# A Mamba block with a gated feed-forward layer: the first layer norm computed transposed, and the last VectorE tap of the convolution given to ScalarE and GpSimd

## The reference

```python
xz = x @ W_in.T; x_ssm, z = split(xz)              # 128 -> 2 x 256 channels
x_ssm = silu(causal_depthwise_conv(x_ssm, 4 taps) + conv_b)
B, C, dt = x_ssm @ W_x.T; dt = softplus(dt * W_dt + b_dt)
h = exp(dt * A) * h + (x_ssm * dt) * B             # scan over 256 positions, 256 channels x 16 states
y = (sum over states of h * C + x_ssm * D) * silu(z)
x = layernorm(x + y @ W_out.T)                     # the first norm, over 128 channels, eps 1e-5
g = silu(x @ w1 * s1) * (x @ w2 * s2)              # 128 -> 512
g = gelu(g @ h1 * s1'); g = gelu(g @ h2 * s2')     # 512 -> 512, twice
x = layernorm(x + g @ w3 * s3)                     # the second norm
```

## Time and profile before

| | |
|---|---|
| median of 3 runs | 1017.27 us (1015.03 to 1018.2) |
| the profiled execution, time | 1015.19 us |
| the profiled execution, span | 1013.3 us |
| busy share: PE, VectorE, ScalarE, GpSimd | 95%, 92%, 86%, 87% |
| granted TensorE clock, mean | 0.98 of full speed |

### The profile page before, as it was taken

How to read it: one execution, slowest core, us unless ns; L and a number is a source line. 1 busy time by engine, 2 the same in 40 slices (tenths; PEclk the granted TensorE clock), 3 DMA queues, 4 the chain that set the end, 5 groups by cost and what they waited for, 6 DMA issues and landing times.

```text
span 1013.3 us, 13725 instructions
## 1 busy us (share of the span) xinstructions
PE 960.7 (95%) x3874; PEld 427.7 (42%) x3874; DVE 931.6 (92%) x1117; ACT 871.7 (86%) x1497; POOL 877.6 (87%) x529
## 2 busy tenths in 40 slices
PE   7947899999999999999999999999999999989998
PEld 3313335353444435344443535344443534434454
DVE  3799999999999999999999999999999999999500
ACT  5396899999999999999999999999999999987341
POOL 3588998989999898999999899999989899979420
PEclk9686999999999999999999999999999999999999
DMA  6969395794939497693949679493939769393000
GB/s 213 246 184 283 100 279 146 203 247 118 285 95 281 123 246 201 161 276 98 279 102 270 163 205 245 125 275 104 296 104 250 197 164 270 98 277 81 1 11 11
DMA packets 110718, 185.18 MB, mean 183 GB/s; under 512 B 12977, under 2 KB 23729, under 8 KB 110641
## 3 DMA queue, kind: packets, MB, share of 16 engines
q1 hardware_dynamic: 110112, 183.98, 68.6%
q10 hardware_dynamic: 528, 0.32, 0.1%
HBM read 162.23 MB, written 22.02 MB: 182 GB/s over the span
## 4 chain that ended last, share of the span: by engine, by line
issue 44%; DVE 41%; PE 10%; POOL 3%; ACT 1%; DVEq 0%; DMA 0%; POOLq 0%; ACTq 0%
DVE hb L865 21%; DVE U L854 16%; PE GY L951 6%; POOL pb L407 2%; DVE gT L805 1%; DVE conv L794 1%; DVE x L810 1%; PE GY L942 1%; PE GY L1008 1%; PE GY L898 1%; ACT dA L515 0%; DMA win_sb<-win_d 0%; PE GY L983 0%; PE GY L958 0%; PE GY L955 0%
## 5 line engine op out<-in xcount | busy, mean ns | idle before, releaser
L407 POOL TENSOR_TENSOR pb<-hb,crep 128x1024 f32<-128x1024 f32 x256 | 602.1, 2367 | 34.8 <-DVE hb L865 30.6
L865 DVE TENSOR_TENSOR_SCAN hb<-dA,U 128x512 f32<-128x512 f32 x512 | 594.3, 1203 | 0.0
L515 ACT ACTIVATE dA<-dtr,negA 128x510 f32<-128x510 f32 x500 | 325.8, 716 | 16.7 <-DVE hb L865 15.1
L854 DVE TENSOR_TENSOR U<-X,xdr 128x512 f32<-128x512 f32 x500 | 318.3, 683 | 0.0
L951 PE MATMUL GY<-g,h_sb 128*128 128x512 f32 x512 | 234.2, 601 | 0.0
L951 PE MATMUL GY<-hid,h_sb 128*128 128x512 f32 x512 | 228.3, 599 | 1.7 <-ACT dts L583 1.0
L951 PEld LDWEIGHTS GY<-g,h_sb 128*128 128x128 f32 x512 | 93.5, 190 | 138.2 <-issue 138.2
L951 PEld LDWEIGHTS GY<-hid,h_sb 128*128 128x128 f32 x512 | 93.8, 190 | 136.5 <-issue 123.0
L942 PE MATMUL GY<-pb,sel_sb 128*32 128x512 f32 x1024 | 138.7, 614 | 11.6 <-POOL pb L407 11.6
L469 POOL TENSOR_TENSOR hid<-hid,g 128x512 f32<-128x512 f32 x64 | 80.6, 1273 | 8.7 <-ACT g L764 8.4
L958 PE MATMUL GY<-x1T,w_sb 128*128 128x512 f32 x128 | 68.2, 614 | 2.0 <-ACT hid L760 1.7
(11 more groups left out here) (135 smaller groups left out, 1068.0 us busy)
## 6 DMA issues: line engine op xcount, KB each, us to landing
dtr<-scr_dt SPq DMA_DIRECT2D x252, 256.0 KB, 8.0
xdr<-scr_xd SPq DMA_DIRECT2D x252, 256.0 KB, 7.7
brep<-scr_rows SPq DMA_DIRECT2D x32, 256.0 KB, 6.6
crep<-scr_rows SPq DMA_DIRECT2D x32, 256.0 KB, 9.1
scr_dt<-dts SPq DMA_DIRECT2D x32, 256.0 KB, 4.9
scr_xd<-xds SPq DMA_DIRECT2D x32, 256.0 KB, 5.1
xres<-xT_d SPq DMA_DIRECT2D x16, 256.0 KB, 9.6
xT_sb<-xT_d SPq DMA_DIRECT2D x15, 256.0 KB, 4.6
```

What stands on the lines that cost most here:

```text
L407: nc.gpsimd.tensor_tensor(pb[:, qs:qs + 2, :], hb[:, hs:hs + 2, :], crep[:, b % 2, g:g + 1, :].to_broadcast([P, 2, TB]), ALU.mult).then_in ...
L515: nc.scalar.activation(halves(dA[:, decay_slot(b, u), :])[:, :, 1:SEQ], halves(BREP[q] if by_product(b, k) else dtr[:, slot, q, :])[:, :, ...
L854: nc.vector.tensor_tensor(U[i][:], X[:], xdr[:, slot, q + i, :], ALU.mult).then_inc(s_u, 1)
L865: nc.vector.tensor_tensor_scan(hb[:, 2 * (v % H_PAIRS) + i, :], dA[:, decay_slot(j, u), :], U[i][:], 0.0, ALU.mult, ALU.add).then_inc(s_h, 1)
```

## The change

The first norm is computed with channels on the partitions. TensorE forms the centred sum as one 128x512 block (three products), ScalarE squares it once into a new buffer xn, TensorE sums the squares over the channels with a matrix of ones (`sum_squares`), ScalarE forms exp(-0.5*ln(var+eps)) in two passes, and VectorE multiplies straight into x1T (`norm1`, at v = 6 between the two products U and the scans). The transposes, the copy of x1T, the four accumulating squares and GpSimd's two steps of the first rsqrt go. The third tap becomes a third scaled copy by ScalarE (into xn) and a third sum by GpSimd; `taps(A)` on VectorE goes. GpSimd does its last output term of a round before the tap sums. The second z product uses another bank and moves up on TensorE; X is refilled at v = 2 where it was v = 3; both copies of z follow the squares; the SiLU of xs moves ahead of the fourth GELU; a table preload follows the first three GELUs of g2.

```diff
@@ -36,7 +36,7 @@
...
-POOL_TAPS = 2
+POOL_TAPS = 3
...
@@ -121,12 +116,11 @@
...
-        xtap0 = [hid[:, 0, :], gT[:, 1, :]]
+        xtap0 = [hid[:, 0, :], gT[:, 1, :], xn[:]]
...
-        var1, ve1, rs1 = sb("var1", [P, NT]), sb("ve1", [P, NT]), sb("rs1", [P, NT])
...
@@ -195,15 +190,18 @@
...
-        BZ = G2
-        BOUT, BX1, BW3 = Y1, Y1, G0
+        def bank_z(b, c):
+            return G0 if c == 1 and b > 2 else G2
+        BOUT, BVAR, BW3 = Y1, G2, G0
...
-        BH2_2 = GY[:, 1:3, :]
+        BH2_2 = (GY[:, 1:3, :],)
...
@@ -497,6 +491,9 @@
...
+                    if v == 15 and intake and back:
+                        for i in range(POOL_TAPS):
+                            add_tap0(I, i)
@@ -537,6 +534,10 @@
...
+                    act.wait_ge(s_x1, b - 2)
+                else:
+                    act.wait_ge(s_wop, 1)
+                    act.wait_ge(s_start, 2)
...
@@ -684,7 +683,7 @@
...
                         softplus_logs(A, 0, lambda: decay(j, 2 * v + AHEAD))
-                    if v == 3 and scan and j > 0:
+                    if v == 2 and scan and j > 0:
                         fill_X(j, 1)
@@ -701,7 +700,9 @@
...
                         act.wait_ge(s_op, F + 1)
-                        variances(x1, lambda t: tile_of(BOUT, t), var1, range(NT), s_var1)
+                        if front:
+                            act.wait_ge(s_tap0, POOL_TAPS * (A - 1))
+                        nc.scalar.activation(xn[:], BOUT, ACT.Square, scale=DM ** -0.5).then_inc(s_sq, 1)
                     if v == 8 and scan and j > 0:
@@ -713,8 +714,9 @@
...
                         if scan:
-                            gelu(g2, flat(BH2_2), s_h2, s_g2, T, 0, 2)
+                            gelu(g2, flat(BH2_2[0]), s_h2, s_g2, T, 0, 2)
                             gelu(g2, BH2[2], s_h2, s_g2, T, 2, 1)
+                            act.preload_act_table_set("natural_log_exp_and_others")
                         else:
@@ -722,18 +724,26 @@
...
                         copy_z(A, 0)
-                    if v == 4 and tail and not front:
-                        for m in ((3,) if scan else (2, 3)):
+                    if v == 4 and tail and not scan:
+                        for m in (2, 3):
                             gelu(g2, BH2[m], s_h2, s_g2, T, m, 1)
+                    if v == (3 if tail else 4) and back and front:
+                        copy_z(A, 1)
                     if v == 5 and front and not back:
...
                         act.preload_act_table_set("natural_log_exp_and_others")
-                    if v == 5 and front:
+                    if v == 5 and front and not back:
                         copy_z(A, 1)
                     if v == 5 and back:
-                        act.wait_ge(s_x1t, F + 1)
-                        nc.scalar.activation(x1T[:, F % 2, :], BX1, ACT.Copy).then_inc(s_x1c, 1)
+                        if front and not tail:
+                            act.preload_act_table_set("natural_log_exp_and_others")
+                        if j == 1:
+                            act.wait_ge(s_zero, 3)
+                        act.wait_ge(s_var1, F + 1)
+                        nc.scalar.activation(xn[:], BVAR, ACT.Ln, bias=eps[:, 0:1]).then_inc(s_ln1, 1)
+                        act.wait_ge(s_ln1, F + 1)
+                        nc.scalar.activation(xn[:], xn[:], ACT.Exp, scale=-0.5).then_inc(s_rs1, 1)
                     if v == 6:
@@ -749,13 +759,13 @@
...
                             nc.scalar.activation(yo[:, 3, :], BLAST[3][:, 0:P], ACT.Copy, scale=rs2[:, 3:4]).then_inc(s_yoa, 1)
-                        if tail and front:
+                        if front and back:
+                            act.wait_ge(s_tap0, POOL_TAPS * (A - 1))
+                            act.wait_ge(*((s_tap1, 3 * A - 6) if tail else (s_conv1, A + 1)))
+                            nc.scalar.activation(flat(xs[:, A % 2, :, :]), flat(conv[:]), ACT.Silu).then_inc(s_xs, 2)
+                        if tail and scan:
                             gelu(g2, BH2[3], s_h2, s_g2, T, 3, 1)
                         for m in range(NH) if back else ():
-                            if m == 1 and front:
-                                act.wait_ge(s_tap, taps_before(A + 1))
-                                act.wait_ge(*((s_tap1, 3 * A - 6) if tail else (s_conv1, A + 1)))
-                                nc.scalar.activation(flat(xs[:, A % 2, :, :]), flat(conv[:]), ACT.Silu).then_inc(s_xs, 2)
                             act.wait_ge(s_ga, 4 * F + 1 + m)
@@ -782,14 +792,11 @@
...
-                moved = POOL_TAPS if b > 1 else 0
-                for s in range(1, TAPS - moved):
+                for s in range(1, TAPS):
...
-                    if moved:
-                        dve.wait_ge(s_tap0, POOL_TAPS * (b - 1))
...
-                        dve.wait_ge(s_tap, taps_before(b) + s - 1)
+                        dve.wait_ge(s_tap, 3 * b + s - 1)
@@ -803,6 +810,10 @@
...
+            def norm1(b):
+                dve.wait_ge(s_rs1, b + 1)
+                nc.vector.tensor_tensor(x1T[:, b % 2, :], BOUT, xn[:], ALU.mult).then_inc(s_x1, 1)
...
@@ -852,6 +861,8 @@
...
                                 nc.vector.tensor_tensor(U[i][:], X[:], xdr[:, slot, q + i, :], ALU.mult).then_inc(s_u, 1)
+                        if v == 6 and back:
+                            norm1(F)
                         if v == 9 and tail:
@@ -866,8 +877,6 @@
...
-                    if v == 1 and front and j > 0:
-                        taps(A)
...
@@ -989,19 +998,15 @@
...
                 pe.wait_ge(s_gate, 2 * b + 2)
-                for t in range(NT):
-                    nc.tensor.matmul(tile_of(BOUT, t), tile_of(xres[:], t), cent[:], start=(t == 0), stop=False, skip_group_check=True)
-                for t in range(NT):
-                    for c in range(NC):
-                        last = nc.tensor.matmul(tile_of(BOUT, t), tile_of(gT[:, c, :], t), wout_sb[:, c, :],
-                                                start=False, stop=(c == NC - 1), skip_group_check=True)
+                nc.tensor.matmul(BOUT, cent[:], xres[:], start=True, stop=False)
+                for c in range(NC):
+                    last = nc.tensor.matmul(BOUT, wout_sb[:, c, :], gT[:, c, :], start=False, stop=(c == NC - 1))
                 last.then_inc(s_op, 1)
-            def turn_x1(b):
-                pe.wait_ge(s_x1, b + 1)
-                for t in range(NT):
-                    last = nc.tensor.transpose(tile_of(BX1, t), x1[:, t, :], ident[:])
-                last.then_inc(s_x1t, 1)
+            def sum_squares(b):
+                pe.wait_ge(s_sq, b + 1)
+                nc.tensor.matmul(BVAR, ones[:].to_broadcast([P, P]), xn[:], start=True, stop=True).then_inc(s_var1, 1)
@@ -1078,21 +1083,31 @@
...
                         z_proj(A, 0)
+                    if v == 3 and tail and front:
+                        pe.wait_ge(s_g2, 4 * T + 3)
+                        z_proj(A, 1)
                     if v == 3 and tail:
...
                         hidden(BH2[3], h2_sb, 3, g1, s_g1, s_h2, T)
-                    if v == (4 if back else 5) and front:
+                    if v == (4 if back else 5) and front and not tail:
                         pe.wait_ge(s_zc, 2 * A + 1)
...
                     if v == 4 and back:
-                        turn_x1(F)
+                        if front:
+                            pe.wait_ge(s_zc, 2 * A + 2)
+                        else:
+                            pe.wait_ge(s_g2, 4 * T + 2)
+                        pe.wait_ge(s_one, 1)
+                        sum_squares(F)
                     if v == 4 and tail:
...
                         else:
+                            if front:
+                                pe.wait_ge(s_zc, 2 * A + 2)
                             add_x1(T)
                     if v == 4 and tail and j <= NB:
-                        down(T, range(NH - 1 if front else NH))
+                        down(T, range(NH - 1 if scan else NH))
                     if v == 12 and intake and not back:
...
```

More of the change, by code:

```diff
@@ L46, in decay_slot @@
     return (TILES * b + u) % DA_RING
-def taps_before(b):
-    return 3 * b if b < 2 else 6 + (3 - POOL_TAPS) * (b - 2)
 def states_of(k):
@@ L109, in build @@
         gT = sb("gT", [P, NC, TB])
-        x1 = sb("x1", [P, NT, DM])
-        wout_raw = x1[:].rearrange("p a b -> p (a b)")[:, 0:DI]
-        diagD = x1[:].rearrange("p (a c) b -> p a c b", a=2)[:, 1, :, :]
+        xn, ones = sb("xn", [P, TB]), sb("ones", [P, 1])
+        wout_raw = xn[:, 0:DI]
+        diagD = xn[:, DI:].rearrange("p (c b) -> p c b", c=NC)
         rep_sb = gT[:, 1, 0:PARITIES * P].rearrange("p (e m) -> p e m", e=PARITIES)
@@ L144, in build @@
         s_warm = sem("s_warm")
+        s_one = sem("s_one")
         s_zero, s_aexp, s_aneg = sem("s_zero"), sem("s_aexp"), sem("s_aneg")
@@ L443, in _ @@
             nc.gpsimd.memset(eps[:], EPS).then_inc(s_zero, 1)
```

(20 more changed lines are left out.)

2 lines of the change are left out of this document (1 added, 1 removed).

## The result

**The changed kernel takes 1037.84 us (median of 4 runs, 1037.03 to 1039.29), the kernel before 1016.15 beside it: a ratio of 1.0216 [1.0199, 1.0233].** The forecast was 1034 with a range of 1012 to 1043. The profiled execution took 1037.18 us with a span of 1035.4, against 1013.3 before. One execution in what follows, of e12, took 1036.05 us with its granted clock at 0.931 where the others had 0.976 to 0.981, and e12's time leaves it out.

The account below looks back on a forecast made before the run. ScalarE and TensorE hand in hand become the bound, at 59.36 us a round against 57.84: +1.52 over 12 rounds is 18.2, with the ends +18.3, so 1015.19 becomes 1033.5, taken as 1034 (range 1012 to 1043).

Parts of the forecast that it names:

- A: ScalarE from the anchor (table load before the SiLU of xs at v = 6) to the softplus: 12.29 becomes 14.48 us.
- B: ScalarE from the softplus to the load before the first GELUs of g2: 30.40 becomes 30.76 us.
- C: ScalarE from the load before the first GELUs of g2 to the refill of X: 5.94 becomes 4.72 us.
- D: ScalarE from the refill of X to the next round's table load at v = 6: 9.21 becomes 9.40 us.
- GpSimd ... priced at nothing: GpSimd's added sum of 1.29 us a round was priced at nothing: 56.3 us of work lies under VectorE's 57.21.
- The square's step: The norm's one square on ScalarE was taken as 0.50 us, between bounds of 0.48 and 0.61.
- the anchor of round 2: Round 2's table load at v = 6 was to come 0.5 us earlier than in the kernel before.
- Behind the last anchor: After the last such load, the norm's product adds 0.6 us; the stretch after the last scan was priced at 0.
- VectorE's idle time: About 2.1 us a round, before the U product of step 4 and at step 12, waiting for ScalarE's X.
- VectorE's floor: Rival, chance 0.16: VectorE stays the bound at 57.21 us a round, giving 1006 us.
- The handshake costs half: Rival, chance 0.12: ScalarE and TensorE wait less at v = 6; round 58.0 to 58.8 us, 1018 to 1027 us.
- Switches close together cost more: Rival, chance 0.04: three nearby table loads cost a further 1.28 us a round, giving 1049 us.

Follow-up runs that it names:

- e12: e9 with the norm's Ln and Exp moved ahead of the last decay of step 5 on ScalarE; 1013.58 us, ratio 0.9966.
- e3: The changed kernel with the third tap given back to VectorE; 1024.33 us, ratio 1.0078.
- e8: The changed kernel with gate 1 waiting for one tap sum instead of three, and round 0's sums behind output term 15; 1034.70 us.
- e7: e1 with gate 1 waiting for one tap sum instead of three, and round 0's sums behind output term 15; 1014.93 us.
- e9: e7 with the table load after the first three GELUs of g2 moved behind the start of Y and the refill of X; 1011.02 us.
- e2: e1 with one extra table load, forced by a one-element exponential between the fourth GELU and SiLU 0; 1033.52 us.
- e6: e1 with the third tap back on VectorE, leaving the transposed norm without the extra table load; 1015.49 us, ratio 0.9990.
- e1: The changed kernel with the SiLU of xs back behind gate pair 0, so seven table loads a round instead of eight; 1017.84 us.
- e4: The kernel before with only the third tap moved (third scaled copy by ScalarE, third sum by GpSimd); 1032.32 us, ratio 1.0145.
- e5: e4 with GpSimd's three tap sums behind output term 15 instead of ahead of it; 1027.85 us, ratio 1.0110.
- e10: The changed kernel with the last part of the down-projection behind up-projection 1 on TensorE; 1057.30 us, ratio 1.0408.

## Why the prediction was right, point by point

**The round.** Forecast 59.36, measured 59.39. Its four parts:

| stretch | forecast | measured | marks of the changed kernel |
|---|---|---|---|
| A, anchor to softplus | 14.48 | 14.16 | 464.21, 478.37 |
| B, to the load before g2 | 30.76 | 30.65 | 509.02 |
| C, to the refill of X | 4.72 | 5.16 | 514.18 |
| D, to the next anchor | 9.40 | 9.42 | 523.60 |

The sum is closer than its parts deserve, which is luck: A came out 0.32 short of its forecast and C 0.44 over. *A* was 0.32 too long. I let up 1 wait for SiLU 0 and start 0.35 behind it, 6.53 after the anchor. SiLU 0 was in time, and up 1 ran on behind gate product 1 without a gap (469.58 + 0.86 = 470.44), 6.23 after the anchor. Up 3 followed 9.75 after the anchor instead of 9.97, and the softplus 4.41 behind it instead of 4.51. *C* was 0.44 too short: the third GELU of g2 waits 0.30 for GpSimd's sum, because the three tap sums now stand ahead of it, and the wait takes away an overlap of 0.11 (the two GELUs take 1.02 + 0.60 apart and 1.51 together in e3). That is the step "GpSimd ... priced at nothing", and it was wrong: I compared GpSimd's work of a whole round with the floor and did not look at its place in the round. e3 shows the term's size (0.41 of the tap's 0.99). The square's step was 0.48, within its bounds of 0.48 and 0.61.

**Start and end.** I said -0.5 at the anchor of round 2; it was +1.9. In round 0 the third sum stands ahead of the output terms for which the first gate waits, which is the same oversight. e8 and e7 do these sums later and give back 3.1 and 2.9 us. Behind the last anchor I had +0.6 and it was +1.6. The missing 1.0 lies behind the last gate of VectorE: 56.7 us (978.72 to 1035.4) where it was 55.7 (957.61 to 1013.3). I had priced one more table load there and called it even. The new form brings two, since no preload stands ahead of the last norm and its logarithm and its exponential each get a load of their own. That these loads are the missing 1.0 is read from the timeline and not tested:

```profile
986.45 1.28 ACT L744 ACT_TABLE_LOAD   x1
...
988.45 1.28 ACT L746 ACT_TABLE_LOAD   x1
```

The misses at the two ends, 2.4 and 1.0 us, are nearly all of the 3.7 between the 1033.5 forecast for the profiled execution and its 1037.18. From there to 1034 the forecast added 0.5, though it named 2.1 as the distance of the median; the measured distance is 0.66.

**The mechanism.** The tests named before came out so: the anchor every 59.4 us (yes), TensorE's wait of about 1.3 for the GELU (1.26), the softplus 14.5 after the anchor (14.16), no wait of ScalarE for a scan (none in the round). VectorE's idle time was forecast at about 2.1 and measured at 1.9 (57.48 busy of 59.39), but it is not where I put it: only 0.1 at the refill of X of step 4 and none at step 12; it stands at the two gates and at the scaling of yo. e8 shows that the place tells nothing of the cause: with gate 1's wait loosened, 0.73 of it is at the refill of X and the round is the same.

**The rivals.** VectorE's floor (1006) was excluded by its gaps, and e9, the best of its kind, still has a round of 57.61. "The handshake costs half" would have been 58.0 to 58.8. It fell because nothing caught up behind the wait: copy 1 still waits 0.24 for up 1, and the softplus waits 0.67 for TensorE where it waited 0.57 before. "Switches close together cost more" fell as well. The Trainium skill, in "ScalarE: Activation LUTs", section "What ACT_TABLE_LOAD costs", has a drain of about 1380 ns with every switch. The trace does not agree: the three loads at v = 6 take 1.30 or less each with the step to their instruction, and e2's added load costs 1.29 us a round.

**What the change is made of.** From e6 the norm's new form costs nothing when the tap stays on VectorE. The other two parts do not simply add up. The four rounds are:

| SiLU of xs | tap on VectorE | tap moved |
|---|---|---|
| behind pair 0 | 57.72 (e6) | 57.82 (e1) |
| ahead of the GELU | 58.40 (e3) | 59.39 (changed) |

With the tap moved, the place of the SiLU is worth 1.57 us a round, as much as the whole change costs in a round, and 1.29 of it is the load that the place brings (e2); with the tap on VectorE it is 0.68, because there VectorE's work alone takes 57.72, and that is the round in e6. The tap's move costs 0.99 where ScalarE sets the round, and 0.1 where it does not, though it takes 0.63 of work from VectorE. What the tap gives VectorE went to waits, first at the gate, then at X's refill, and came back in small part when a load was put behind that refill (e9).

## What to carry to other kernels

Don't read an engine's slack over the whole round: GpSimd had 3 us free and the third tap still cost 0.99 us a round (e4). Look at the place where each piece of new work goes in, on every engine that gets one. Moving GpSimd's three sums alone gave back only 0.15 (e5), since ScalarE's third copy and the refill and the norm behind it were late as well. A switch of tables costs its load where the engine's order is on the ring, so group by table, and put copies, which need none, ahead of the load rather than behind it. The largest gap of the fastest engine need not be what costs time: loosen its wait first and see if the period moves.

## What the runs showed that I had not expected

- TensorE's granted clock fell to 0.50 in the middle of eight steady rounds of e10 after idle times of 1.17 and 0.78 us with one product between them, and was back at 1.00 some 3.4 us later. That cost 1.6 to 1.7 us of slower products in such a round. In five other rounds of the same execution the same two idle times left it at 1.00, and so did the one idle time of 1.26 in the changed kernel. So the fall came behind these waits in some rounds and not in others; what decides it is not shown here.
- An activation of one element takes 0.20 us between two loads, with steps of 0.01 or 0.02.
- Ln and Exp one exponential earlier (e12) took away the only wait of VectorE that e9's timeline showed, and the round did not get shorter (57.74 against 57.61). The 95% intervals of the two ratios, [0.9953, 0.9979] and [0.9939, 0.9967], overlap, so which is faster stays open.
